# VectorE's share of the score comparisons in a graph attention kernel as one-source operations, without the edge bytes

## The reference

```
Wh = (x @ W.T).reshape(n, 4, 32).transpose(1, 0, 2)
e = leaky_relu(score_src + score_dst, 0.2)      # [4, n, n], score_src = Wh.a1, score_dst = Wh.a2
e = where((adj == 0)[None], -inf, e)
alpha = softmax(e, axis=-1)
h_prime = einsum('kij,kjd->kid', alpha, Wh)     # [4, n, 32]
out = layernorm(x + h_prime.transpose(1, 0, 2).reshape(n, 128), eps=1e-5)
```

## Time and profile before

| What | Value |
|---|---|
| Median of 3 runs | 1601.66 us (1600.64 to 1603.05) |
| Profiled execution: span from its first to its last instruction | 1599.2 us |
| VectorE busy | 1545.1 us |
| ScalarE busy | 1496.1 us |
| TensorE busy | 1421.6 us |
| GpSimd busy | 1382.8 us |
| One group of 16 quads in groups 1 to 14 (1288 us over 14) | 92.0 us |

### The profile page before, as it was taken

How to read it: one execution, slowest core, us unless ns; L and a number is a source line. 1 busy time by engine, 2 the same in 40 slices (tenths; PEclk the granted TensorE clock), 3 DMA queues, 4 the chain that set the end, 5 groups by cost and what they waited for, 6 DMA issues and landing times.

```text
span 1599.2 us, 77812 instructions
## 1 busy us (share of the span) xinstructions
PE 1421.6 (89%) x35205; PEld 1388.1 (87%) x35205; DVE 1545.1 (97%) x2156; ACT 1496.1 (94%) x1834; POOL 1382.8 (86%) x1495
## 2 busy tenths in 40 slices
PE   6058999999999999999999999999999999999995
PEld 6048899989989999998999999898999989989995
DVE  7978999999999999999999999999999999999995
ACT  3799999999999999999999999999999999999883
POOL 1798898988989899898989899898989989998994
PEclk9579999999999999999999999999999999999998
DMA  4235565756666575666656666665666566565650
GB/s 161 88 118 183 179 213 172 232 184 194 212 194 213 173 234 193 203 194 211 207 179 220 196 203 200 200 220 174 225 200 199 190 204 232 170 212 188 200 187 22
DMA packets 162564, 303.01 MB, mean 189 GB/s; under 512 B 10296, under 2 KB 22968, under 8 KB 162232
## 3 DMA queue, kind: packets, MB, share of 16 engines
q1 hardware_dynamic: 162232, 298.03, 57.6%
HBM read 293.67 MB, written 4.33 MB: 186 GB/s over the span
## 4 chain that ended last, share of the span: by engine, by line
ACT 48%; DVE 29%; PE 14%; issue 5%; POOL 4%; DMA 0%; SPq 0%; POOLq 0%; DVEq 0%; ACTq 0%
ACT kept L471 35%; PE bank L783 12%; ACT step L471 9%; DVE rest L667 7%; DVE step L638 6%; DVE rest L665 5%; DVE kept L657 4%; DVE step L652 2%; ACT late L498 2%; PE bank L770 2%; ACT y L504 1%; POOL kept L407 1%; DVE step L650 1%; POOL G L411 1%; DVE stats L693 1%
## 5 line engine op out<-in xcount | busy, mean ns | idle before, releaser
L471 ACT ACTIVATE kept<-s_two,sd 128x1024 uint8<-128x1024 f32 (+1 forms) x1024 | 1066.7, 1122 | 39.4 <-PE bank L783 36.6
L421 POOL TENSOR_SCALAR step<-s_own,sd 128x512 uint8<-128x512 f32 x1040 | 704.7, 699 | 2.4
L783 PE MATMUL bank<-G,kept 128*128 128x99 bf16 x8192 | 535.9, 207 | 23.4 <-issue 14.6
L351 POOL TENSOR_SCALAR edge<-adj_t 128x2048 int8<-128x2048 int32 x256 | 485.2, 1895 | 77.3 <-PE bank L770 57.7
L783 PE MATMUL bank<-F,rest 128*128 128x66 f16 x16384 | 548.6, 194 | 3.0 <-issue 2.9
L783 PE MATMUL bank<-G,step 128*128 128x99 bf16 x8192 | 536.3, 207 | 9.6 <-issue 9.4
L783 PEld LDWEIGHTS bank<-F,rest 128*128 128x128 fp8e4 x16384 | 529.1, 98 | 2.9 <-issue 2.8
L783 PEld LDWEIGHTS bank<-G,kept 128*128 128x128 fp8e4 x8192 | 415.9, 97 | 31.1 <-issue 17.6
L783 PEld LDWEIGHTS bank<-G,step 128*128 128x128 fp8e4 x8192 | 420.2, 97 | 13.1 <-issue 12.8
L638 DVE SCALAR_TENSOR_TENSOR step<-s_own,sd,bank 128x512 uint8<-128x512 f32 x496 | 348.6, 746 | 7.0 <-PE bank L770 6.4
L471 ACT ACTIVATE step<-s_own,sd 128x512 uint8<-128x512 f32 x512 | 341.5, 721 | 0.0
(11 more groups left out here) (82 smaller groups left out, 549.9 us busy)
## 6 DMA issues: line engine op xcount, KB each, us to landing
adj_t<-in_adj SPq DMA_DIRECT2D x512, 512.0 KB, 4.8
s_own<-sT_scratch SPq DMA_DIRECT2D x32, 256.0 KB, 5.9
s_two<-sT_scratch SPq DMA_DIRECT2D x31, 256.0 KB, 5.1
kept<-in_x SPq DMA_DIRECT2D x16, 256.0 KB, 5.9
y<-in_x SPq DMA_DIRECT2D x16, 256.0 KB, 5.4
out<-y SPq DMA_DIRECT2D x16, 256.0 KB, 5.2
y<-sT_scratch SPq DMA_DIRECT2D x1, 256.0 KB, 3.8
sT_scratch<-late SPq DMA_DIRECT2D x2, 64.0 KB, 1.9
```

What stands on the lines that cost most here:

```text
L351: nc.gpsimd.tensor_scalar(edge[:, k % N8], adj_t[:, k % NA], 1.0, -1.0, ALU.min, ALU.max).then_inc(edge_set, 1)
L421: last = nc.gpsimd.tensor_scalar(step_u8[:, k % NS, h - KEPT, n // E, :, n % E], s_own[:, g % 2, h - KEPT], STEEP, d_steep[:, q * IB + n, ...
L471: return nc.scalar.activation(out, scores, ACT.Sigmoid, scale=STEEP, bias=d_steep[:, q * IB + b, h:h + 1])
L783: last = nc.tensor.matmul(acc[k][:, col:col + width], matrices[h][:, n // E, b * P:(b + 1) * P, n % E], values[:, q * IB + n, h].rearrange ...
```

## The change

VectorE's comparisons no longer read the transposed edges. They become one-source operations on the scores in SBUF with a scalar for each partition, and no longer wait for TensorE's transposes, but for their slot of `step` to be free, as those of ScalarE and GpSimd do. The wait for the transposes moves to `take_step`, which now ands all words of `step` in one instruction for every quad.

```
--- before.py
+++ after.py
@@ -154,7 +154,6 @@
         wide_G, wide_F = ([acc[2 * n + k][:, 0:TJ * HEADS * HC].rearrange("p (j h c) -> p j h c", h=HEADS, c=HC)
                            for n in range(NU)] for k in range(2))
         edgeT16 = [t[:, :].bitcast(bf16).rearrange("p (u i) -> p u i", u=U) for t in tr]
-        edgeT8 = [t[:, :].bitcast(i8).rearrange("p (u i e) -> p u i e", u=U, e=E) for t in tr]
         edgeT = [t[:, :].bitcast(i32).unsqueeze(1).to_broadcast([P, 2, WORDS]) for t in tr]
 
         sT = nc.dram_tensor("sT_scratch", [HEADS, N], fp32, kind="Internal").ap()
@@ -633,11 +632,11 @@
                 k = quad_no(g, q)
                 if q == 0:
                     dve.wait_ge(own_loaded[g % 2], 32 * (g // 2 + 1))
-                dve.wait_ge(transposed, k + 1)
+                if k >= NS:
+                    dve.wait_ge(rest_done, k - NS + 1)
                 for b, h in tiles(g, q)[2]:
-                    last = nc.vector.scalar_tensor_tensor(step_u8[:, k % NS, h - KEPT, b // E, :, b % E], s_own[:, g % 2, h - KEPT],
-                                                          d_neg[:, q * IB + b, h:h + 1], edgeT8[q % 2][:, b // E, :, b % E],
-                                                          ALU.is_ge, ALU.logical_and)
+                    last = nc.vector.tensor_scalar(step_u8[:, k % NS, h - KEPT, b // E, :, b % E], s_own[:, g % 2, h - KEPT],
+                                                   d_neg[:, q * IB + b, h:h + 1], None, ALU.is_ge)
                 last.then_inc(dve_compared, 1)
 
             def take_step(g, q):
@@ -646,14 +645,9 @@
                 dve.wait_ge(dve_compared, k + 1)
                 dve.wait_ge(act_compared, k + 1)
                 dve.wait_ge(pool_compared, k + 1)
-                if len(tiles(g, q)[2]) == E:
-                    nc.vector.scalar_tensor_tensor(step[:, k % NS, 1, 0:WORDS // U], edgeT[q % 2][:, 1, 0:WORDS // U], ONES,
-                                                   step[:, k % NS, 1, 0:WORDS // U], ALU.bitwise_and, ALU.bitwise_and)
-                    nc.vector.scalar_tensor_tensor(step[:, k % NS, 0], edgeT[q % 2][:, 0], ONES,
-                                                   step[:, k % NS, 0], ALU.bitwise_and, ALU.bitwise_and)
-                else:
-                    nc.vector.scalar_tensor_tensor(step[:, k % NS], edgeT[q % 2], ONES,
-                                                   step[:, k % NS], ALU.bitwise_and, ALU.bitwise_and)
+                dve.wait_ge(transposed, k + 1)
+                nc.vector.scalar_tensor_tensor(step[:, k % NS], edgeT[q % 2], ONES,
+                                               step[:, k % NS], ALU.bitwise_and, ALU.bitwise_and)
                 nc.vector.scalar_tensor_tensor(kept[:, both(k, k)[0]], edgeT[q % 2], ONES, kept[:, both(k, k)[0]],
                                                ALU.bitwise_and, ALU.bitwise_and).then_inc(step_set, 1)
```

## The result

The changed kernel takes 1758.9 us (1758.5 to 1759.3, 4 runs) beside 1602.4 us for the kernel before: a ratio of 1.098, interval 1.096 to 1.099, or 156.5 us more. The forecast was 1663 us, 61 us more. The sign was right and the time lies inside the stated range of 1600 to 1775 us, but the change is 2.6 times as large as forecast.

The account below looks back on a forecast made before the run. VectorE was taken as the bound: -0.54, +0.20 and +0.6 us make +0.26 a quad, +58 us over 224 quads, +3 for group 15. With 61 on 1599.2 and 2.5 more: 1663 us, range 1600 to 1775.

Parts of the forecast that it names:

- The bound: Groups 1 to 14: VectorE bounds, at 91.5 of 92.0 us a group, with ScalarE 1.8 us behind the 92.0.
- The comparison itself: VectorE's one-source comparison takes 477 ns, 0.385 us from start to start; two save 0.54 us a quad.
- no doubled rate: Rival: VectorE's byte output with gaps runs one column a cycle, without conflict; 1618 to 1647, middle 1630 us; chance 0.13.
- The and over all words: In `take_step`, one instruction of 1024 words costs 1.13 us where two cost 0.93: +0.20 us a quad.
- The moved waits at nothing: VectorE's wait for transposes, moved to `take_step`, and its new wait for TensorE's F products cost 0.
- The groups outside 1 to 14: Group 0 is ScalarE's and adds 0; group 15, with one comparison a quad, adds 3 us.
- That the conflict arises: VectorE's doubled-rate comparison collides with GpSimd's work, as line 600's two SBUF sources do in the preamble.
- The price of the conflict: VectorE waits for the rest of GpSimd's instruction: 0.6 us a pair, between 0.4 and 1.0; chance of one wait 0.54.
- The pair is split: Rival: GpSimd gets in between VectorE's two comparisons; second wait at least 0.55 us, 123 us more, 1786 us; chance 0.18.
- GpSimd's loss: GpSimd loses the time of VectorE's pair, 0.6 to 0.8 us a quad: 93.6 us a group, VectorE still the bound.
- The signs named for it: GpSimd's line 421 rises from 699 to some 800 ns, line 351 above 1895; waits for lines 702 and 688 shrink.

Follow-up runs that it names:

- the run as one instruction: The changed kernel with VectorE's two comparisons of a quad made into one instruction of 1024 columns, wrong threshold for the second tile: 1647.4 us, 1.029.
- the two-source run: The changed kernel with the scores in SBUF as second source of VectorE's comparisons too, so they run one column a cycle: 1883.8 us, 1.176.
- the comparisons apart: The changed kernel with the second comparison of a quad moved between the two instructions of `take_rest`: 1656.2 us, 1.034.
- The runs with one tile: The changed kernel, GpSimd comparing one of four tiles from group 1 on: 1764.3 us; the same with VectorE's comparisons behind `take_rest`: 1594.4 us.
- the version with the free places: The changed kernel with VectorE's order and on `kept`, and on `step`, rest of `kept`, first comparison, rest of `step`, second comparison: 1654.8 us, 1.032.

## Why the prediction was right or wrong

**The bound** was right. VectorE is idle for 6.4 us of the stretch of 1288 us before the change and for 1.7 us after it, and every 0.1 us a quad on it is 22 us of the kernel.

**The comparison itself** was right: 474 ns undisturbed for 477. In the run as one instruction 512 more columns cost 270 ns, where 256 more cost 266 at the single rate, so the doubled rate holds for a byte output with gaps. The rival "no doubled rate" is out.

**The and over all words** was right: +46.6 us in its own run for 224 x 0.20 = 45.

**The moved waits at nothing** was right. There is no idle time ahead of line 638.

**The groups outside 1 to 14** were right: nothing for group 0 and 3 us for group 15, where the trace has 2 and 3. The reading behind the first was loose, since of the 15.7 us of idle time ahead of line 650 the row gives 5.5 to ScalarE and 9.7 to "issue".

**That the conflict arises** was right, from line 600 alone, and the Trainium skill (SBUF — State Buffer, Who interferes with whom) has it for the one-source form too. This trace and the two-source run agree with it (0.508 and 0.505 us of wait).

**The price of the conflict** is the step that failed: "Between 0.4 and 1.0 I take 0.6 us for a pair". It measures 1.02 us, just outside the bounds that the prediction gave as the sign of being wrong. Two things were wrong in it. First, I took one wait for a pair. The trace after shows two, with one GpSimd instruction let in between, as the rival "The pair is split" had it: a mean of 0.33 us for the first comparison and 0.70 for the second. The first wait alone was priced too high. The second, which the forecast put at nothing, is the larger. That rival gave 1786 us; the measured time is nearer to it (27 us) than to my forecast (96 us). It lies below the rival and inside the range only because the first wait came out at 0.33 in place of 0.6 us, which is luck and not a right step: the range was meant to leave most of the split pairs out. The rival took at least 0.55 us for the second wait, from a comparison of GpSimd; the trace has closing pieces and whole conversions there too, which make it 0.70. Its row was in the earlier trace rows, the one at 46.08 us, and I weighed it against the row at 55.22, where VectorE kept both turns. The runs with the comparisons apart and as one instruction take 103 and 111 us off.

Second, I averaged over arrivals at random, though I had the phase of one quad beside it. The arrival is not random: `rest_set` releases the transposes, those release the conversion, and the comparisons stand 2.2 us behind `rest_set` on VectorE. I had computed this phase for the first comparison (0.43 us; the timeline after shows 0.35), and did not see that GpSimd's next instruction stands ready behind the conversion and goes in before the second. The runs with one tile show it: 1764 us in one place, 1594 in another.

**GpSimd's loss** was too high. I had 0.6 to 0.8 us a quad. Over the whole kernel it is busy 1455.5 us, its waits for VectorE included, against 1382.8: 0.28 us a quad. The comparisons' share is 4 x 39 ns, and the closing piece of line 377 rose from 1348 to 1493 ns. In the stretch of 1288 us it is busy 1092.6 us against 1153.0, so a larger share of its time is idle than before. The signs named for it (line 421, now 420, at some 800 ns with single ones near 1300; line 351, now 350, well above 1895 ns; shorter waits for lines 688 and 702, now 682 and 696) did not come: 738 ns with a longest of 987, 1911 ns, and waits of 51.1 and 59.2 us.

What stays open is the rule by which VectorE keeps its turn or loses it between two instructions: in the earlier trace rows it kept it at 54.74 and lost it at 46.08. In groups 1 to 14 of the changed kernel VectorE lost the turn at all 192 pairs where GpSimd had an instruction ready, and no run varied the distance between the two neighbours.

## What to carry to other kernels

A faster form of an instruction can need a path that another engine uses. Its own duration is then the smaller part of its price: here 0.54 us a quad were gained and 1.02 lost. Price a held resource per instruction, not per block of work, since the other engine gets in between two neighbours; and before averaging a wait, follow the semaphores to see whether one event starts both sides, because then the collision repeats in every round. Moving the instruction is the test: if the same work costs another time in another place, the place has a part in it. Load can have one too: behind `take_rest` the wait for a pair was 0.12 us with one tile on GpSimd and 0.54 with four.

## What was not expected of the hardware

An instruction that waits for the semaphore of the one just before it on VectorE starts 0.12 us later than one whose semaphore is an instruction older (1.44 against 1.31 us and 1.24 against 1.13 in the kernel before, with its comparisons behind `take_rest`). The whole kernel took 50 us longer, and two such places in 224 quads account for 54. That the neighbouring semaphore is the reason was read from the order and not tested by itself; the version with the free places has no such pair and fits its sum without the 0.24 us. GpSimd's conversion in four instructions of 512 elements takes 610 ns each in the median, 643 in the mean with their waits, and costs more than one of 2048 at 1892 to 1911 ns.
